# One kernel of attention and a Fourier mixer: second-half pieces set ahead of the weighted sum, some pieces at other steps, and one transfer issued earlier

## What is computed

```python
x = x + attention(group_norm(x), w_qkv, w_o)       # 12 heads of 16, 1024 tokens an image
x = x + mixer(group_norm(x), w1, b1, w2, b2, bias_w, bias_b)

def attention(x):
    q, k, v = split(tokens(x) @ w_qkv)             # (b, 12, 1024, 16) each
    p = softmax(einsum('bhqd,bhkd->bhqk', q, k) * 16 ** -0.5)
    return merge_heads(einsum('bhqk,bhkd->bhqd', p, v)) @ w_o

def mixer(x):
    f = rfftn(blocks_of_48(x), axes=(H, W), norm='ortho')
    h = relu(complex_mul(f, w1) + b1); g = complex_mul(h, w2) + b2   # 4 blocks of 48
    return irfftn(g) + x @ bias_w.T + bias_b
```

## Time and profile before

| | |
|---|---|
| median of 3 runs | 1496.27 us (1491.05 to 1497.83) |
| profiled execution | 1497.2 us |
| its span | 1495.3 us |
| busy: PE, DVE, ACT, POOL | 95%, 77%, 68%, 13% |
| the eight bodies | from 81.2 us to about 1417 us |
| granted TensorE clock, mean | 0.977 |

### The profile page before, as it was taken

One profiled execution on the slowest core, in us unless ns is written; L12 is line 12 of the kernel. 1 busy time (PEld: TensorE's weight loads), 2 busy tenths in 40 slices (PEclk: granted clock), 3 DMA queues, 4 the chain that ended last, 5 costly groups with the idle time before them and its releaser, 6 DMA issues.

```text
span 1495.3 us, 27421 instructions
## 1 busy us (share of the span) xinstructions
PE 1425.8 (95%) x9986; PEld 683.4 (46%) x9986; DVE 1158.1 (77%) x2155; ACT 1009.6 (68%) x2018; POOL 187.5 (13%) x277
## 2 busy tenths in 40 slices
PE   7699989899999999999999999999999999999988
PEld 4344333444545454444445454444545454434455
DVE  3687888788798878998798878998799978988041
ACT  1055777577776777677776777677777777677712
POOL 2000000130010300130010400121000400030000
PEclk7789999999999999999999999999999999999999
DMA  4430312313323414413322414413323324311213
GB/s 115 75 65 2 86 33 60 63 55 79 86 70 72 97 52 82 108 48 83 88 65 68 103 50 89 107 42 79 87 56 67 98 55 88 86 50 45 62 43 87
DMA packets 100463, 106.37 MB, mean 71 GB/s; under 512 B 24745, under 2 KB 77417, under 8 KB 100329
## 3 DMA queue, kind: packets, MB, share of 16 engines
q1 hardware_dynamic: 98616, 103.19, 30.1%
q10 hardware_dynamic: 1712, 1.43, 0.4%
HBM read 26.99 MB, written 6.67 MB: 23 GB/s over the span
## 4 chain that ended last, share of the span: by engine, by line
PE 79%; DVE 7%; DMA 6%; POOL 2%; issue 2%; SPq 2%; ACT 1%; ACTq 0%; DVEq 0%; POOLq 0%
PE o_acc L1288 21%; PE ring L1267 15%; PE scores L1235 14%; PE ring L1311 10%; DVE row_max L1033 5%; DMA inv_all<-inv_rows 4%; PE ring L1300 3%; PE ring L1424 2%; PE ring L1411 2%; PE ring L1417 2%; PE ring L1403 2%; PE scores L1311 1%; SPq L703 1%; POOL inv_all L577 1%; PE ring L1322 1%
## 5 line engine op out<-in xcount | busy, mean ns | idle before, releaser
L1033 DVE TENSOR_REDUCE row_max<-ring 128x1 f32<-128x512 f32 x1536 | 974.8, 682 | 181.6 <-PE ring L1267 175.2
L930 ACT ACTIVATE probs<-scores 128x512 f32<-128x512 f32 x1536 | 828.8, 600 | 271.1 <-PE scores L1235 270.2
L1267 PE MATMUL ring<-k_stack,q_stack 48*128 48x512 f32 x1536 | 589.1, 465 | 27.5 <-DVE row_max L1033 24.9
L1235 PE MATMUL scores<-q_stack,k_stack 50*128 50x512 f32 x1536 | 594.2, 460 | 2.6 <-DMA q_stack<-shift 1.3
L1288 PE MATMUL o_acc<-probs,v_aug 128*18 128x512 f32 x3072 | 407.5, 603 | 2.4 <-ACT probs L930 1.2
L1235 PEld LDWEIGHTS scores<-q_stack,k_stack 50*128 50x128 f32 x1536 | 244.0, 186 | 317.6 <-ACT probs L930 300.5
L1267 PEld LDWEIGHTS ring<-k_stack,q_stack 48*128 48x128 f32 x1536 | 246.1, 188 | 147.1 <-DVE row_max L1033 99.2
L577 POOL TENSOR_TENSOR inv_all<-o_raw,inv_all 128x1024 f32<-128x1024 f32 x23 | 54.5, 2371 | 585.8 <-DMA inv_all<-inv_rows 585.8
L1288 PEld LDWEIGHTS o_acc<-probs,v_aug 128*18 128x18 f32 x3072 | 51.9, 96 | 123.2 <-issue 87.8
L1311 PE MATMUL ring<-xt,w_qk 64*128 64x256 f32 x504 | 62.3, 379 | 0.0
L1311 PEld LDWEIGHTS ring<-xt,w_qk 64*128 64x128 f32 x504 | 48.8, 186 | 9.0 <-DVE row_max L1033 3.8
(11 more groups left out here) (158 smaller groups left out, 1097.8 us busy)
## 6 DMA issues: line engine op xcount, KB each, us to landing
q_stack<-qk_parts SPq DMA_DIRECT2D x288, 64.0 KB, 2.2
k_stack<-qk_parts SPq DMA_DIRECT2D x144, 128.0 KB, 4.2
inv_all<-inv_rows SPq DMA_DIRECT2D x23, 512.0 KB
rows_b<-rows_a SPq DMA_DIRECT2D x122, 96.0 KB, 2.8
x_in<-in_x_dram SPq DMA_DIRECT2D x8, 768.0 KB, 5.0
x_res<-in_x_dram SPq DMA_DIRECT2D x8, 768.0 KB, 4.7
spec_b<-spec_a SPq DMA_DIRECT2D x60, 102.0 KB, 2.3
o_t<-inv_all SPq DMA_DIRECT2D x184, 32.0 KB, 1.9
```

What stands on the lines that cost most here:

```text
L930: nc.scalar.activation(probs[:, GH * (s % 2) + h, :], scores[:, n % SCORE_BANKS, :], ACT.Exp, scale=SCALE).then_inc(probs_made, 1)
L1033: nc.vector.tensor_reduce(row_max[:, which, m:m + 1], max_bank(g, unit, i), AX.X, ALU.max).then_inc(max_taken, 1)
L1235: mm(scores[:, n % SCORE_BANKS, :], k_stack[rows, 2 * g + hp, P * kt:P * (kt + 1)], q_stack[rows, g, half, hp, :], start=True, stop=True). ...
L1267: mm(max_bank(g, unit, i), q_stack[rows, g, half, hp, P * qt:P * (qt + 1)], k_stack[rows, 2 * g + hp, HALF * which:HALF * (which + 1)], st ...
```

## The change

Three things are changed. On PE the MID pieces stand ahead of `pv` instead of behind it. Some pieces have other steps or other halves of a step. And `SPREAD_AT` and `PACK_AT` are 2 and 6 in place of 5 and 7, `TOKENS_AT` and `PLACE_V_AT` have other steps.

```diff
@@ PREP_AT
-    19: ([('qk', 2)], []),
+    20: ([('qk', 2)], []),
-    32: ([('qk', 5)], [('v', 0)]),
-    37: ([], [('v', 1)]),
-    39: ([('v', 2)], []),
-    47: ([('v', 3)], [])}
+    32: ([('qk', 5)], []),
+    34: ([('v', 0)], []),
+    39: ([('v', 1)], []),
+    40: ([], [('v', 2)]),
+    45: ([], [('v', 3)])}
@@ POST_AT
-    27: ([], [('dftw', 2)]),
-    28: ([('dftw', 3)], []),
+    28: ([('dftw', 2), ('dftw', 3)], []),
-    44: ([('lin', 2)], []),
+    47: ([('lin', 2)], []),
-    50: ([('lin', 3)], []),
-    53: ([('idftw', 0)], []),
-    54: ([], [('idftw', 1)]),
-    55: ([('idftw', 2)], [('idftw', 3)])}
+    51: ([('lin', 3)], []),
+    53: ([('idftw', 0)], [('idftw', 1)]),
+    55: ([], [('idftw', 2)]),
+    56: ([('idftw', 3)], [])}
-POST_FOLLOW = {..., 26: [('normalise', 0), ('normalise', 1)], 27: [('normalise', 2)]}
+POST_FOLLOW = {..., 21: [('normalise', 0)], 26: [('normalise', 1), ('normalise', 2)]}
-PLACE_V_AT = {26: 2, 40: 0, 45: 1}
-TOKENS_AT = {20: (0,), 21: (1,), 24: (2,), 27: (3,), 28: (4,), 30: (5,)}
+PLACE_V_AT = {26: 2, 42: 0, 45: 1}
+TOKENS_AT = {20: (0,), 21: (1,), 24: (2,), 28: (3,), 31: (4,), 34: (5,)}
-SPREAD_AT = 5
+SPREAD_AT = 2
-PACK_AT = 7
+PACK_AT = 6
@@ PE, body
                     score_tile(b, g, s, 1)
+                    pieces(u, MID)
                     if s > 0:
                         pv(b, g, s - 1)
...
-                    pieces(u, MID)
                     score_tile(b, g, s, 2)
```

More of the change, by code:

```diff
@@ L88 @@
     42: ([('mix2', 4)], []),
-    44: ([('lin', 2)], []),
     45: ([('idfth', 0), ('idfth', 1), ('idfth', 2)], []),
     46: ([('idfth', 3)], []),
-    50: ([('lin', 3)], []),
-    53: ([('idftw', 0)], []),
-    54: ([], [('idftw', 1)]),
-    55: ([('idftw', 2)], [('idftw', 3)])}
+    47: ([('lin', 2)], []),
[3 more added lines that the diff above has]
+    56: ([('idftw', 3)], [])}
 PREP_FOLLOW = {0: [('stats', 0)], 3: [('stats', 1)], 6: [('stats', 2)], 7: [('gather', 0)], 12: [('normalise', 0)], 13: [('normalise', 1)], 14: [('normalise', 2)]}
-POST_FOLLOW = {14: [('stats', 0)], 15: [('stats', 1)], 16: [('stats', 2), ('gather', 0)], 26: [('normalise', 0), ('normalise', 1)], 27: [('normalise', 2)]}
-PLACE_V_AT = {26: 2, 40: 0, 45: 1}
-TOKENS_AT = {20: (0,), 21: (1,), 24: (2,), 27: (3,), 28: (4,), 30: (5,)}
+POST_FOLLOW = {14: [('stats', 0)], 15: [('stats', 1)], 16: [('stats', 2), ('gather', 0)], 21: [('normalise', 0)], 26: [('normalise', 1), ('normalise', 2)]}
+PLACE_V_AT = {26: 2, 42: 0, 45: 1}
+TOKENS_AT = {20: (0,), 21: (1,), 24: (2,), 28: (3,), 31: (4,), 34: (5,)}
 STACK_AT = {10: 'q1', 11: 'q0', 13: 'k'}
 INVERT_AT = 2
-SPREAD_AT = 5
+SPREAD_AT = 2
 SUMS_DOWN_AT = 0
 SUMS_BACK_AT = 0
-PACK_AT = 7
+PACK_AT = 6
 RESIDUAL_AT = 17
```

## The result

| | before | after |
|---|---|---|
| median of the runs | 1496.88 us (6 runs) | 1511.07 us (6 runs) |
| range | 1491.05 to 1503.27 | 1505.24 to 1518.15 |
| profiled execution: span | 1495.3 us | 1514.2 us |
| its mean granted clock | 0.977 | 0.967 |

The account below looks back on a forecast made before the run. PE (95% busy) was taken as the bound, so only its waits or lower clock could be won: 6.3 + 0.8 + 1.2 + 0 + 1.0 + 0.3 = 9.6 us less, forecast 1487 us, range for 8 in 10 1480 to 1496.

Parts of the forecast that it names:

- Term 1: SP's spreading read goes ahead of the image load: all five PE waits for `o_t` vanish, 6.3 us gained.
- The shift's wait: PE's 1.32 us wait in body 1 for the shift: to shrink by about 0.8 us, between 0 and 1.3.
- Term 2: Clock of body 1: without the 2.85 us wait it has no reason to fall, 1.2 us gained, between 0 and 1.4.
- Term 3: Pieces moved to other steps: six empty steps per full body before and after, so zero change.
- DVE in steps 20 to 22: Rival: bodies 1 to 7 lose 1.4 us each there, steps 2 to 4 as much again: 1506 us, chance 0.12.
- Term 4: MID pieces ahead of `pv`: banks filled before it and emptied during it, 1.0 us gained, between -1 and 3.
- Term 5: `lin 2` in step 47 instead of 44, in the last body's ACT-paced end: 0.3 us gained, between -0.5 and 1.

Follow-up runs that it names:

- S: Before with only the order on SP changed (SPREAD_AT = 2, PACK_AT = 6, spreading read ahead of the image load): 1492.86 us, ratio 0.9956.
- S M: Before with the new SP read order and the MID pieces ahead of `pv`, old tables: 1519.35 us, ratio 1.0131.
- the extra matmuls: Twelve unused 128x256 matmuls in empty ring banks of body 0, added to after: 1505.74 us; added to the kernel with S alone: 1491.86 us.
- T: Before with only the new tables of steps (both tables, `POST_FOLLOW`, `PLACE_V_AT`, `TOKENS_AT`): 1512.46 us, ratio 1.0094.
- S T: Before with the new SP read order and the new tables, MID pieces still behind `pv`: 1505.46 us, ratio 1.0040.
- M: Before with only the MID pieces moved ahead of `pv`: 1520.82 us, ratio 1.0140.
- two halves of T: S with only the new tables of steps 18 to 31: 1500.60 us; S with only those of steps 32 to 47: 1500.14 us.

## Why the prediction was wrong

**Term 1 held** (-6.3 us forecast; bodies 1 to 5 are 5.7 us shorter with S alone). Its working was too simple: the read was slowed to 9.8 us, so the pack came 2.3 us sooner in body 4, not 3.8. That is still more than four of the five waits were long, and of the fifth, 2.85 us, 0.4 stayed. The shift's wait stayed 1.3 us in after, where 0.8 less was forecast (0.8 us long with S alone, 2.5 with S M).

**Term 2** (-1.2) came true in body 1 by luck. In after the clock no longer falls there, but the reason given, "Without the 2.85 us wait the clock has no reason to fall there", is refuted: with S alone the wait is gone, and body 1 has 10.2 us at half clock instead of 3.4; so it is in five of the other kernels with S. And body 0 lost far more, which no term had. The text priced the clock where a long wait stood and never asked how long body 0, which lacks the second half's pieces and waits for DVE 23 times (11.4 us in before), stays at the lower level. It is between 12 and 49 us in the profiled executions of this study. After's runs have 87 us at half clock on average, before's 73: at 0.34 us each some 5 us of the 15. With the extra matmuls after has 67.

**Term 3 failed first: "six and six. ... I take zero."** Counting empty steps left out which step the piece goes to. It costs 1.17 us per body: 0.62 in steps 18 to 31 and 0.56 in steps 32 to 47, 7 us in bodies 1 to 6, and nothing in steps 1 to 8, where the differences sum to 0.01. The rival "DVE in steps 20 to 22" named the right place and was given too little: it was to cost 1.4 us per body and cost 0.73. The argument against it, idle time of DVE in sum, was the wrong test; DVE had 1.8 us idle in the same stretch while PE waited for it. The second half of the loss no rival had. Some 0.4 us per body of it are `v 3` behind `pv` in step 45 (1.23 against 0.84 us), against the sentence "A piece costs PE the same anywhere"; 0.2 us are step 44, which became empty and waits for ACT, where the prediction had counted empty steps as waits for DVE alone.

**Term 4 failed in its sign: "banks are filled before `pv` and emptied during it"** (-1.0 us). It looked at the input of a MID piece, found 1.2 us left in step 30, and did not look at its bank. With the new tables that costs 0.31 us per body, 1.9 us; with the old ones it would have been 21. That the tables and the move belong together could have been read from the diff: exactly the pairs `qk 2` with `var`, `qk 5` with `v 0`, `qk 4` with `dftw 2` were taken out of one step.

**Term 5** (-0.3): body 7 is 0.8 us longer in after. Not tried by itself.

The sum by the runs, at equal time at half clock: S -5.3; T +10.7 (S T against S; 7 us of it are the steps of bodies 1 to 6, some 2 body 0, which is 3.0 us longer with 2.4 us more at half clock, 0.5 body 7, the rest isn't placed); M +2.5 (1.9 us by the steps); together 7.9 us, and 5 us for the clock, 13 of the 14 us between the medians. The two halves of T measured apart, 5.1 and 6.1 us over S, add up to about the same. What stays open is which part lowers the clock, and whether one does: T alone has 87 us at half clock, S T 75, after 87, and single runs of one kernel lie up to 60 us apart. The means of after and of S T have a standard error of 5 us each, so their difference of 12 can be chance.

## What to carry to other kernels

Before a piece is moved, ask three things of its new place: who still holds its buffer there and what work covered that wait, how late the slowest engine already is in that very step (idle time summed over five steps says nothing), and whether its neighbours on the array use the same halves. Changes to a schedule that were made together must be priced together: the move ahead of `pv` costs 3.5 us per body with one table and 0.3 with another. Where an engine's clock follows its load, as the extra matmuls show here, look for the stretch in which the engine is thinly used, and give it a term of its own.

## What the hardware showed unexpectedly

- A broadcast read of 512 KB with a 768 KB load close behind on the same queue took 9.8 instead of 7.4 us (body 4), and the load 10.3 instead of 5.0 (medians).
- The clock fell to half for 10.2 us in body 1 of the kernel with S alone, where PE's last wait had been 0.77 us; in before it fell there for 3.4 us, behind a wait of 2.85 us.
- Twelve matmuls of no use brought the time at half clock from 71 to 55 us with S alone, where the gain (1491.86 against 1492.86 us) is within the noise, and from 87 to 67 us in the changed kernel, which became 5 us faster by the medians (1505.74 against 1511.07 us).
- The twelve matmuls of a 64-row pair took 0.84 us between tiles of two halves, and 0.95 us behind a full-height weighted sum, with another 0.28 us in what followed (step 45).
